# Gated cross-attention and a routed expert block: slot tiles listed in three segments instead of two, with the scatters, weight loads and variances around them moved

## The reference

```python
def attn(q, k, mask, pad, qc, Wq, bq, Wk, bk):
    qp, kp = q @ Wq.T + bq, k @ Wk.T + bk               # 128 features
    s = qp @ kp.T * 128**-0.5 * qc
    return softmax(where(mask | pad, -inf, s))
def ffn(h, Wg, W1, W2, W3, bias):                       # h: [2048, 512]
    r = sigmoid(h @ Wg.T)
    top = top_k(r + bias, 2)                            # two experts a token
    w = r[top] / sum(r[top])
    g = silu(h @ W1[e].T) * (h @ W3[e].T) * w[e]        # of the chosen two
    return sum_e g @ W2[e].T
x = x + tanh(g_xattn) * attn(ctx, ctx, mask, pad, layernorm(x), Wq, bq, Wk, bk)
x = x + tanh(g_ffn) * ffn(layernorm(x), Wg, W1, W2, W3, bias)
```

## Time and profile before

| | us |
|---|---|
| median of 3 runs | 348.43 (347.24 to 350.96) |
| profiled execution, its own time | 343.01 |
| its span, first to last instruction | 341.2 |
| PE busy | 281.3 |
| DVE busy | 193.1 |
| ACT busy | 127.5 |
| POOL busy | 189.3 |
| mean granted TensorE clock | 0.905 of full |

### The profile page before, as it was taken

How to read it: one execution, slowest core, us unless ns; L and a number is a source line. 1 busy time by engine, 2 the same in 40 slices (tenths; PEclk the granted TensorE clock), 3 DMA queues, 4 the chain that set the end, 5 groups by cost and what they waited for, 6 DMA issues and landing times.

```text
span 341.2 us, 5162 instructions
## 1 busy us (share of the span) xinstructions
PE 281.3 (82%) x1311; PEld 205.6 (60%) x1316; DVE 193.1 (57%) x495; ACT 127.5 (37%) x239; POOL 189.3 (55%) x192
## 2 busy tenths in 40 slices
PE   3689985699637229679979999999999999999980
PEld 1134552344323227468857888888888888888860
DVE  3696969987999405963433454454545444454430
ACT  2677764447316514031321333223332333323320
POOL 4196987187744633176785554556545635654313
PEclk9989998569878557898997999999999999999997
DMA  7997988469995234244795666467666555865344
GB/s 225 318 404 283 306 316 270 142 161 158 204 205 133 61 97 121 62 61 66 68 107 89 113 122 117 77 119 128 121 101 119 107 108 78 158 104 102 55 62 61
DMA packets 27026, 48.69 MB, mean 143 GB/s; under 512 B 9524, under 2 KB 10296, under 8 KB 25976
## 3 DMA queue, kind: packets, MB, share of 16 engines
q0 software_dynamic: 9760, 20.49, 36.5%
q1 hardware_dynamic: 14408, 15.04, 14.8%
q10 hardware_dynamic: 2832, 12.85, 13.5%
HBM read 28.51 MB, written 19.85 MB: 142 GB/s over the span
## 4 chain that ended last, share of the span: by engine, by line
DMA 41%; issue 24%; POOL 12%; DVE 9%; PE 8%; POOLq 2%; ACT 1%; SPq 1%; ACTq 0%
DMA out<-rows,slot 28%; DMA out<-rows 8%; POOL rows L435 5%; POOL out L454 3%; POOL slot_table L422 3%; PE bank L888 2%; PE bank L910 2%; DMA rows<-in_x 1%; DMA rows<-xn_rows,slot 1%; DMA w_hi<-in_ctx_t 1%; PE bank L927 1%; POOLq L446 1%; DMA slot_table<-entry,slot_index 1%; DVE rows L687 1%; PE bank L895 1%
## 5 line engine op out<-in xcount | busy, mean ns | idle before, releaser
L454 POOL DMA_INDIRECT out<-rows,slot x39 | 62.0, 1590 | 71.8 <-DMA out<-rows,slot 36.8
L977 PE MATMUL bank<-w_hi,xt_hi 128*128 x156 | 66.3, 425 | 0.1
L805 DVE TENSOR_TENSOR xt_lo<-bank,xt_hi 128x512 fp32r<-128x512 f32 x39 | 27.0, 692 | 66.4 <-ACT xt_hi L577 66.4
L978 PE MATMUL bank<-w_lo,xt_hi 128*128 x156 | 62.3, 400 | 0.0
L979 PE MATMUL bank<-w_hi,xt_lo 128*128 x156 | 61.9, 397 | 0.0
L435 POOL DMA_INDIRECT rows<-xn_rows,slot x39 | 39.1, 1003 | 22.4 <-issue 16.7
L598 ACT ACTIVATE rows<-bank,slot 128x512 f32<-128x512 f32 x39 | 26.8, 687 | 53.9 <-PE bank L1006 44.4
L585 ACT ACTIVATE rows<-bank 128x256 f32<-128x256 f32 x39 | 15.0, 384 | 85.3 <-PE bank L979 85.3
L422 POOL DMA_INDIRECT slot_table<-entry,slot_index x32 | 33.1, 1034 | 20.0 <-issue 13.1
L811 DVE SCALAR_TENSOR_TENSOR rows<-rows,bank 128x256 f32<-128x256 f32 x39 | 16.4, 420 | 42.4 <-ACT rows L585 42.3
L1004 PE MATMUL bank<-w_hi,gt_hi 128*128 x78 | 31.4, 402 | 5.6 <-DVE gt_lo L822 5.6
(11 more groups left out here) (128 smaller groups left out, 447.9 us busy)
## 6 DMA issues: line engine op xcount, KB each, us to landing
w_lo<-in_w ACTq DMA_DIRECT2D x8, 1024.0 KB, 6.6
xn_rows<-w_hi SPq DMA_DIRECT2D x17, 256.0 KB, 5.7
rows<-in_x SPq DMA_DIRECT2D x16, 256.0 KB, 4.5
out<-rows SPq DMA_DIRECT2D x16, 256.0 KB, 6.4
w_lo<-in_w ACTq DMA_DIRECT2D x8, 512.0 KB, 12.1
w_hi<-in_ctx_t SPq DMA_DIRECT2D x4, 256.0 KB, 4.1
slot<-slot_table SPq DMA_DIRECT2D x39, 1.0 KB, 2.0
rows<-xn_rows,slot POOLq DMA_INDIRECT x39, 4.3
```

Source lines behind the costliest of these rows:

```text
L454: pool.indirect_dma_start(out=out[0:SPARE + P * READY[segment(i)], :], out_offset=bass.IndirectOffsetOnAxis(ap=slot[:, i, 0:1].bitcast(U32 ...
L805: dve.tensor_tensor(xt_lo[:, i % 2].rearrange("p k s -> p (k s)"), ps_x[i % 2][:], xt_hi[:, i % 2].rearrange("p k s -> p (k s)").bitcast(F32),
L977: pe.matmul(ps_h[i % 2][:], xt_hi[:, i % 2, k, :], hi, start=(k == 0), stop=False)
L978: pe.matmul(ps_h[i % 2][:], xt_hi[:, i % 2, k, :], lo, start=False, stop=False)
```

## The change

It has five parts.

- The groups of the router become 6, 6 and 4 row tiles (before 6, 4 and 6), and the list has three segments of 5, 12 and 22 slot tiles, from 6, 12 and 16 row tiles. Segment 0 rests on group 0, segment 1 on groups 0 and 1, segment 2 on all.
- DVE makes the list of segment 0 at step 8 with the slots of group 0. Group 1 is ranked at step 13 (before 11) and gets its slots at step 14 (before 12); its list comes behind the last weight split, before the first gate. Group 2's ranks, weights, slots and list follow the gated transposes of slots 1, 2, 3 and 4 (before: ranks ahead of slot 0's gate, weights and slots in slot 0, the list in slot 1). PE counts its positions in slot 2 instead of 1.
- The scatters of group 1 are issued four at step 15, four behind normed(15) and four behind gather(4) (before: eight, at steps 13 and 14). Those of group 2 are eight at slots 6 to 9 (before twelve at slots 1 to 7).
- Loads 7 to 15 are issued at steps 6 to 12, with three of them at step 8, instead of steps 7 to 12 with two at each of the last three.
- The instruction of line 659, which scales the first variance, moves from DVE to POOL's `row_scales`. Small buffers of the list now lie inside `compared`, and `slots_all` is the buffer `sc`.

The diff, cut to what changes:

```diff
     XG = 3
-    GROUPS = (6, 4, 6)
-    START = (0, 6, 10)
-    END = (6, 10, 16)
+    GROUPS = (6, 6, 4)
+    START = (0, 6, 12)
+    END = (6, 12, 16)
     MOST = max(GROUPS)
-    SEGMENTS = (13, LIST - 13)
-    FIRST = (0, 13, LIST)
-    READY = (10, TILES)
+    SEGMENTS = (5, 12, LIST - 17)
+    FIRST = (0, 5, 17, LIST)
+    READY = (6, 12, TILES)
     UNITS = 3 * E
...
     LO_BY_POOL = (0, 1, 2, 4, 6, 7, 9, 10)
-    LOADS = {0: (2,), 1: (3,), 2: (4,), 4: (5,), 5: (6,), 7: (7,), 8: (8,), 9: (9,), 10: (10, 11), 11: (12, 13), 12: (14, 15)}
-    SCATTERS = {9: (0, 0, 3), 10: (0, 3, 6), 11: (0, 6, 9), 12: (0, 9, 12), 13: (1, 0, 4), 14: (1, 4, 8)}
-    LATE_SCATTERS = {1: (2, 0, 2), 2: (2, 2, 4), 3: (2, 4, 6), 4: (2, 6, 8), 5: (2, 8, 10), 6: (2, 10, 11), 7: (2, 11, 12)}
+    LOADS = {0: (2,), 1: (3,), 2: (4,), 4: (5,), 5: (6,), 6: (7,), 7: (8,), 8: (9, 10, 11), 9: (12,), 10: (13,), 11: (14,),
+             12: (15,)}
+    SCATTERS = {9: (0, 0, 3), 10: (0, 3, 6), 11: (0, 6, 9), 12: (0, 9, 12), 15: (1, 0, 4)}
+    LATE_SCATTERS = {0: (1, 8, 12), 6: (2, 0, 2), 7: (2, 2, 4), 8: (2, 4, 6), 9: (2, 6, 8)}
     SPINS = 5
...
         wts = sb("wts", [P, MOST, E])
-        slots_all = sb("slots_all", [P, MOST, E])
+        slots_all = sc
         is_choice = sb("is_choice", [P, MOST, 2, E])
...
 
-        n_tiles = sb("n_tiles", [P, E])
-        unused = sb("unused", [P, E])
-        tiles_up_to = sb("tiles_up_to", [P, E])
-        taken = sb("taken", [P, E])
         used = sb("used", [P, len(SEGMENTS), E])
-        row_step = sb("row_step", [P, E - 1])
-        first_row = sb("first_row", [P, SEGMENTS[-1]])
-        row_sum = sb("row_sum", [P, SEGMENTS[-1]])
         compared_f32 = compared[:].rearrange("p c t e f -> p (c t e f)").bitcast(F32)
...
         passed = compared_f32[:, 0:SEGMENTS[-1] * (E - 1)].rearrange("p (i e) -> p i e", e=E - 1)
+        small = [compared_f32[:, 200 + 8 * n:208 + 8 * n] for n in range(5)]
+        n_tiles, unused, tiles_up_to, taken = small[0:4]
+        row_step = small[4][:, 0:E - 1]
+        first_row = compared_f32[:, 240:240 + SEGMENTS[-1]]
+        row_sum = compared_f32[:, 280:280 + SEGMENTS[-1]]
         list_expert = sb("list_expert", [P, LIST], I32)
...
         CONSTS = 13
-        EXPERTS_LISTED = (1, 4)
-        ROWS_LISTED = (2, 5)
-        LANDED_LISTED = (3, 6)
+        EXPERTS_LISTED = (1, 4, 7)
+        ROWS_LISTED = (2, 5, 8)
+        LANDED_LISTED = (3, 6, 9)
 
...
                     sp.wait_ge(s_slot_in[i % SLOT_SEMS], 16 * (i // SLOT_SEMS))
-                if i >= FIRST[1] + 4:
+                if i >= FIRST[2] + 4:
                     sp.wait_ge(s_x, i - 8)
...
                         load_slots(i)
-            listed(1)
-            for i in range(FIRST[1], LIST):
-                load_slots(i)
+            for k in (1, 2):
+                listed(k)
+                for i in range(FIRST[k], FIRST[k + 1]):
+                    load_slots(i)
 
...
                 if first:
+                    pool.wait_ge(s_mv1, step + 3)
+                    pool.tensor_scalar(variances[:, ring, 0:1], mv1[:, ring, 1:2], EPS, float(P), ALU.add,
+                                       ALU.mult).then_inc(s_ve1, 1)
                     pool.wait_ge(s_ve1, step + 3)
...
             normed(TILES - 1)
+            enter_slots(1, 4, 8)
             gather(2)
...
                 exponentials(step)
-                g = group_ending(step - 2)
-                if g is not None:
-                    router_tanh(g)
+                if step == END[0] + 1:
+                    router_tanh(0)
+                elif step == END[1] + 1:
+                    router_tanh(1)
                 for unit in units_in(step):
...
             split_hi(UNITS - 1)
-            router_tanh(len(GROUPS) - 1)
             for i in range(LIST):
...
                     gathered_hi(i + 2)
+                if i == 0:
+                    router_tanh(2)
             weighted_rows(LIST - 1)
...
                 dve.bn_aggr(mv1[:, tile % NT, :], bn1[:, tile % NT, :]).then_inc(s_mv1, 1)
-                dve.wait_ge(s_mv1, tile + 1)
-                dve.tensor_scalar(variances[:, tile % NT, 0:1], mv1[:, col, 1], EPS, float(P), ALU.add, ALU.mult).then_inc(s_ve1, 1)
 
...
                 residual(step)
-                g = group_ending(step - 3)
-                if g is not None:
-                    router_slots(g)
-                    if END[g] in READY:
-                        list_tiles(READY.index(END[g]))
-                g = group_ending(step - 2)
-                if g is not None:
-                    router_ranks(g)
-                    router_weights(g)
+                if step == END[0] + 1:
+                    router_ranks(0)
+                    router_weights(0)
+                elif step == END[0] + 2:
+                    router_slots(0)
+                    list_tiles(0)
+                elif step == END[1] + 1:
+                    router_ranks(1)
+                    router_weights(1)
+                elif step == END[1] + 2:
+                    router_slots(1)
             for unit in units_in(TILES - 1):
...
             split_lo(UNITS - 1)
-            last = len(GROUPS) - 1
-            router_ranks(last)
+            list_tiles(1)
             for i in range(LIST):
...
                     gathered_lo(i + 2)
-                if i == 0:
-                    router_weights(last)
                 gated_transposed(i)
-                if i == 0:
-                    router_slots(last)
-                elif i == 1:
-                    list_tiles(1)
+                if i == 1:
+                    router_ranks(2)
+                elif i == 2:
+                    router_weights(2)
+                elif i == 3:
+                    router_slots(2)
+                elif i == 4:
+                    list_tiles(2)
 
...
                     pe.wait_ge(s_slots, 4)
-                    pe.wait_ge(s_ls, 1)
+                    pe.wait_ge(s_ls, LS + 1)
                 for k in range(KC):
...
                     masks(step + 1)
-                g = group_ending(step - 3)
-                if g is not None:
-                    positions(g)
+                if step == END[0] + 2:
+                    positions(0)
+                elif step == END[1] + 2:
+                    positions(1)
                 if step < TILES - 2:
...
                     gate_transpose(0)
-                    positions(len(GROUPS) - 1)
                     gathered(3)
...
                         gathered(i + 2)
+                    if i == 2:
+                        positions(2)
                     gate_transpose(i)
...
             output(LIST - 1, last)
```

More of the change, by code:

```diff
@@ L177, in flamingo_routed_block @@
         ps_neg, ps_t, ps_early, ps_q, ps_k, ps_l = bank[2:]
-        ps_pos = (ps_early[:, 0:(MOST + 1) * E], ps_early[:, 0:(MOST + 1) * E], ps_l[:, 2 * P:2 * P + (MOST + 1) * E])
+        ps_pos = 2 * (ps_early[:, 0:(MOST + 1) * E],) + (ps_l[:, 2 * P:2 * P + (MOST + 1) * E],)
         ps_h = bank[0:2]
```

## The result

| | before | changed kernel |
|---|---|---|
| median of 20 runs each, us | 347.82 (343.99 to 351.48) | 349.36 (347.40 to 352.91) |
| profiled execution, its own time | 343.01 | 349.13 |
| its span | 341.2 | 347.2 |
| hidden(0) starts | 130.8 | 127.7 |
| slot 9 starts | 188.3 | 183.6 |

The changed kernel is slower: 1.0117 times before, 95% interval 1.0074 to 1.0159. This ratio leaves out disturbed runs, which is why it is larger than that of the two medians. The forecast was 343.1 us. The time is inside the range of 336 to 352, but the change goes the other way: near 1% slower instead of 1.5% faster.

What follows compares the result with a forecast made beforehand. PE was taken to bound the 39 gathered slots but not the attention and router steps. 343.0 less 8.1 us at slot 0 plus 2.8 given back in the slots made 337.7 profiled, 343.1 as run median; range 336 to 352.

Steps and rivals of the forecast that it cites:

- squares(14): Last squares ahead of slot 0, done at 110.4 before: 2.2 us earlier, bounds 1.1 later and 4.7 earlier.
- Behind it all as before: Slot 0: after gather(0) at 115.9, 8.1 us earlier, the rest takes as long as before, so hidden(0) at 122.7.
- DVE in the steps: Attention and router steps: router pieces cost 1.1 us, variances save 1.5, waits for exponentials save 1.8.
- PE catches up there: Step 8: the 4.2 us list on DVE lets PE catch up, saving 1.8 us of waits for exponentials.
- The moved instruction of the variance: Attention and router steps: taking it off DVE saves 0.2 us at seven of thirteen places, 1.5 us, bounds 0 and 2.9.
- gather(2): Slots 0 to 1: behind four scatters, its rows come after PE wants them, 3.1 us lost.
- The list at slot 4: Slot 4: the list takes 3.5 us of DVE, and 3.9 of PE with the half clock behind it.
- gather(5): Waits for segment 1, goes at +21.1 after hidden(0), just hidden; add(0) behind it costs 1.7 us and 1.4 in its wake.
- eight late scatters at slots 6 to 9 instead of twelve at 1 to 7: Gathered slots: these scatters, 2.6 us of POOL a slot, lose 1.5 us.
- B: Slots 0 to 12: late gather(5) and waits for adds cancel slot 0's gain; 22.5 lost, 348 us, no change; chance 0.23.
- A: Transition to slots: scatters stall in issuing and land 1.7 us later; slower, 357 us, or 352 with two blocks; chance 0.15.
- C: First slots: stalls overlap rather than add up, 11 us lost instead of 17.5; more gained, 335.6 us; chance 0.20.

Runs made afterwards that it cites:

- the second trace: The changed kernel run once more, unchanged, on the same chip as a second run of the kernel before: 345.03 us, 1.0116 of before.
- the trace with a late store: The kernel before with five more waits for the add ahead to land, at slots 4, 5, 6, 9 and 14: 1.0139 of before.

## Why the prediction was wrong

**Where slot 0 was wrong.** The forecast had hidden(0) at 122.7, and it came at 127.7 in the first trace and 126.2 in the second. Three terms, by the first trace: squares(14) ended at 109.5, 0.8 us earlier and not 2.2; the four scatters of step 15 took 6.7 us and not 5.4; and gather(0) landed in 6.4 us and not in 3.5. The last is the largest, and the second trace has it too (6.4), while squares(14) ended 2.2 us earlier there, as forecast. "Behind it all as before" was the step: before had gathered from an empty queue, since SyncE's wait had made sure that all scatters had landed. The change took away that wait and with it the empty queue. With gather(0) ahead of the scatters it landed in 4.4.

**DVE in the steps.** "PE catches up there" did not happen in the first trace. Timelines of PE (910 and 911 add the masks) and DVE in the changed kernel:

```profile
61.97 0.61 PE L910 MATMUL bank<-w_hi,ident_bf 128*128 128x512 bf16 x1 [5.55 <-DVE zmax L672]
...
71.36 0.61 PE L910 MATMUL bank<-w_hi,ident_bf 128*128 128x512 bf16 x1 [2.05 <-DVE zmax L672]
...
79.86 0.63 PE L910 MATMUL bank<-w_hi,ident_bf 128*128 128x512 bf16 x1
...
87.78 0.38 PE L910 MATMUL bank<-w_hi,ident_bf 128*128 128x512 bf16 x1
...
87.59 0.16 DVE L687 RECIPROCAL rden<-prob_sum 128x1 f32<-128x1 f32 x1 [3.52 <-ACT bank L529]
```

The same matmul takes 0.61 to 0.63 us at 62, 71 and 80, and 0.38 at 88. The granted clock was 0.5 of full (1.2 GHz) from 57.1 to 67.3, full up to 70.7, and 0.5 again up to 84.4; before it was 0.5 from 57.6 to 74.7 and then full. PE at half clock was then late in project(3), its last projection, and DVE waited 3.52 us for the exponential; its waits of this kind sum to 5.6 us, where I had counted on saving 1.8 of 5.4. The second trace of the same kernel has it the other way. Its timeline of PE, and the sum of these waits (us, times, longest):

```profile
71.01 0.61 PE L910 MATMUL bank<-w_hi,ident_bf 128*128 128x512 bf16 x1 [0.28 <-DVE zmax L672]
...
77.66 0.38 PE L910 MATMUL bank<-w_hi,ident_bf 128*128 128x512 bf16 x1
...
DVE rden L687 <- ACT bank L529: 2.4, 5, 1.5
```

The clock was full from 74.5 on, DVE waited 2.4 us in all, 3.0 less than before, and squares(14) came as early as forecast. So this step failed in one execution and held in the other. What tells them apart is not shown: a second gap on PE (2.05 us at 71, against 0.28) is in the first alone, but in the run with spread scatters the gap is 0.29 and the clock still stays at 0.5 up to 84.3. The moved instruction of the variance was worth nothing that the runs show, instead of 1.5.

**Where the slots were wrong.** 17.5 us lost were forecast, 23.4 and 19.1 came. gather(2): 3.1 forecast, 5.4 measured (slots 0 to 1 took 10.2 us), by its landing of 8.91 us. The list at slot 4, with 3.9, was too dear: 1.8 (slots 5 to 6 took 6.5). gather(5) was forecast well, +21.1 against +21.8, but the 3.1 us (1.7 and 1.4 in its wake) for add(0) behind it did not come: ACT scales slot 2 at 156.84 after 0.98 us of idle time, for PE, and slots 3 and 4 take 4.8 us each. And the step that decided the sign: "eight late scatters at slots 6 to 9 instead of twelve at 1 to 7: 1.5". It is 8 to 10 in slots 9 to 14. The twelve of before could have warned: taking them out won 7.6 us of lost time, and 4.9 of that stand in its first trace at slots 7 to 9. I had taken 4.8 us for an add and 3.5 for a gather everywhere, the one a median over 39, the other from the one gather with nothing ahead. The trace of before had the other values: its chain of waits shows 6.21 and 5.89 us for the adds at 147.5 and 154.6, with scatters ahead, and 4.6 to 5.3 behind 184.

**The rivals.** B had the mechanism in part: "the waits for adds run on through slots 5 to 12", POOL's slot too long. It made it a matter of POOL's issue time (5.8 us against 4.75), and forecast no change. The rows show landing, not issue: spreading the scatters leaves POOL's total issue time as it is and takes about half of the loss in slots 9 to 14. A had the scatters around the transition as what decides, but by stalls in issuing (one of 3.57 us was there) and by 1.7 us more for the scatters' own landing, not by what they do to the DMA behind them. A's scatter median of 7.5 us was the hint. That the time lay inside the range is not to the forecast's credit: the range came from A and C, and the forecast's own mechanism would have made the kernel faster.

**Landing times.** The Trainium skill, DMA: Bandwidth & Descriptors, Anatomy of one DMA — SWDGE (gpsimd) path, has some 2 us for a small DMA. This case's runs don't agree for the indirect DMAs: the scatter of 1 KB that the prediction priced took 5.8 us, with scatters ahead of it, and the 256 KB ones take 3.5 us (gather) and 4.6 (add) with nothing ahead, up to 9.5 with scatters ahead. The same page of the Trainium skill, Issuing engines are not separate DMA queues, says that DMAs of all issuing engines interleave on the same 16 DMA engines. What counted here was narrower: the order within POOL's own queue. As to the shared SBUF interfaces (the Trainium skill, GPSIMD Engine Reference, Specifications): moving the thirteen instructions back changed nothing that could be measured, in either direction.

**What was right.** The wait of SyncE went and gather(0) no longer depended on it. gather(2) was late, gather(5) waited 8.3 us for its slot with add(0) behind it, the loads made no difference, and the pitch behind was 4.75.

**What stays open.** Why the first part varies by 5 us between runs, in both kernels; the trace with a late store is one instance. Why gather(0) takes 0.9 us longer than before even with no scatter near it. And how the queue lengthens a landing: these runs show that and how much, not what happens inside.

## What to carry to other kernels

A wait that holds a DMA back until a queue is empty also gives it a short landing; when you take the wait away, price the DMA with what now stands ahead of it in its queue. Read a landing in the neighbourhood in question, with and without others ahead, not from a median. And spread small indirect DMAs one by one between large ones: eight of them moved by a few slots took the kernel from 1.012 to 0.986 of before here, 5 us by the medians and 9 by the ratios.

## What the runs showed that I had not expected

- A scatter of 128 entries of 8 bytes, 1 KB in all, delays a gather or an add of 256 KB behind it. Adds take 4.6 to 5.3 us with nothing ahead, 4.8 to 6.1 with one scatter and 5.9 to 9.5 with two, the longest behind an add that had not landed; gathers take 3.5 to 4.5 with none and 6.4 and 8.9 behind four. That is, as an estimate from these, up to 1.5 us a scatter.
- Five waits for landings cost 1.2 us where no late scatters are and 5.9 where they are. With one trace to each corner the difference is a hint only.
- Two executions of one kernel can differ by 10 us in how long TensorE stays at half clock (to 74.5 or to 84.4 us), with hidden(0) 1.5 us apart.
